# Expert tiles of a graph-plus-mixture kernel: rows scaled by rows and turned by transposing DMAs, gathers issued ahead of additions

## The chip, the cores and the metric

One core of one Trainium2 chip runs the whole program in one launch. The metric is the device time of one execution in microseconds; the median of three runs of the kernel before is 1963.51 us (1962.75 to 1968.17).

## The reference

Three blocks run over the same 6250 nodes of 256 features: a graph attention over 100000 edges, a linear attention, and a mixture of 8 experts of which each node uses 2. The change touches the last block only. Cut to what matters there:

```python
# x: (6250, 256), N = 6250, D = 256, 8 experts, H = 1024
xn = (xt - mu) * rsqrt(var + 1e-5)                 # one row per node
xe = xn[None] * ln_g[:, None] + ln_b[:, None]      # the scale and shift belong to the expert
h = gelu(einsum('end,edh->enh', xe, W1) + b1[:, None])
y = einsum('enh,ehd->end', h, W2) + b2[:, None]
out = (weights[:, :, None] * y[token, its 2 experts]).sum(1)
```

Here `xt` is itself a layer norm of x, so that two norms follow each other; the kernel does both at once and leaves the result in HBM as `xn2_d`.

## The kernel before, in words

The kernel first walks the edges and does the linear attention beside it (up to about 1200 us of the span), then norms all nodes, picks two experts per node and sorts the node-expert pairs by expert. What follows, from about 1322 us on, is the expert loop, and everything below is about it.

The pairs, padded per expert, are cut into FT = 56 tiles of FR = 256 rows; a tile belongs to one expert e. All weights W1 and W2 lie in SBUF, each split into a high and a low float16 part. The activations are split in the same way, so a product takes three float16 products. Even tiles use buffer u = 0 and odd ones u = 1.

For a tile s, in order:

- **GpSimd** (`pool_turn`, the block `@block.gpsimd`) copies the row numbers of turn i into `now` (`places_now`, L857), then issues indirect DMAs. In turn i it adds the gated answers of tile i - 5 to `out` (`add_rows`, L862, two DMAs of 128 rows that read, add and write; the second waits until the first has landed, because the two may hit the same node), gathers the gates of tile i - 2 (`get_gates`, L867, two DMAs) and gathers the 256 normed rows of tile i (`get_rows`, L873, two DMAs into `rows_s`). The order within a turn is: wait until tile i - 2 has been turned by TensorE, wait until tile i - 5 is gated, wait for the additions of the turn before, copy, first addition, gates, second addition, rows.
- **TensorE** (`pe_turn_rows`, L2229) transposes the rows of tile s + 1 in four 128x128 float32 pieces into PSUM bank 6 or 7. In `pe_tile(s)` it does this first, then `pe_up(s)` (L2243, 48 matmuls, W1 times the activations), then `pe_down(s - 1)` (L2263, 48 matmuls, W2).
- **VectorE** (`dve_affine`, L1890) reads that bank and applies the scale and the shift of the expert, which in this layout are one number per partition (`params_s`, loaded and turned at the kernel's start), into `x_f`. **ScalarE** (`act_high`, L1173) casts `x_f` to float16, the high part; VectorE subtracts it (L1895) for the low part. Both go to `x_hl`, which `pe_up` reads.
- ScalarE applies gelu in four quarters (L1152); VectorE splits each quarter into high and low (L1910, L1911) for `pe_down`; VectorE adds the bias b2 to the answer (`dve_answer`, L1924) and ScalarE multiplies it by the gate (`act_gate`, L1165) into `gated_s`.

VectorE's program order in tile s - 1 is: answer of tile s - 3 (the end of its tile s - 2), then affine and low part of tile s, then the four quarters of tile s - 1. ScalarE's is: gate of tile s - 3, high part of tile s, the four gelu quarters. The order is written out by hand on every engine, with semaphores counted by tile. SyncE issues nothing in the loop: its last DMA stores the gates (L728), and then it waits for the end.

Of the kernel before, what the change touches and what calls it, by code (L numbers as in the profile page):

```python
# [5 lines left out]
ACT = mybir.ActivationFunctionType  # L6
# [3 lines left out]
P = 128  # L10
# [26 lines left out]
FR = 2 * P  # L37
# [103 lines left out]
def build(nc, x, src, dst, gnn_w, attn_l, attn_r, gnn_bias, wq, bq, wk, bk, wv, bv, wo, bo,  # L141
          wr, br, ln_g, ln_b, w1, b1, w2, b2, out):
    ctx = ExitStack()
    with ctx:
# [51 lines left out]
        param_rows = first([98, P])  # L196
# [84 lines left out]
        params = sb("params", [P, 98])  # L281
        b1T, gT, bT, bqT = params[:, 0:64], params[:, 64:80], params[:, 80:96], params[:, 96:98]
# [47 lines left out]
        params_s = params[:, 64:96]  # L330
# [28 lines left out]
        x_f = ffn([P, 2, KD, FR])  # L359
# [77 lines left out]
        def high_hots_of(t0, t1):  # L437
# [62 lines left out]
        place_turn, table_turn, map_turn, places_ready = sem("place_turn"), sem("table_turn"), sem("map_turn"), sem("places_ready")  # L500
        now_ready = sem("now_ready")
        adds_ready, tau_turn = sem("adds_ready"), sem("tau_turn")
        rows_got = [sem(f"rows_got{u}") for u in range(2)]
        gates_got = [sem(f"gates_got{u}") for u in range(2)]
        rows_turned, x_turn, x_high, h_made, gelu_ready, h_turn, y_made, y_ready, y_gated, y_added = (
            sem("rows_turned"), sem("x_turn"), sem("x_high"), sem("h_made"), sem("gelu_ready"), sem("h_turn"),
# [9 lines left out]
        RANKS = 21  # L516

# [27 lines left out]
        def _(sp):  # L545
# [180 lines left out]
            load_w2(7)  # L726
            sp.wait_ge(gates_ready, 1)
            sp.dma_start(gate_d.rearrange("(p t) e -> p t e", t=T), gates[:, :, :]).then_inc(gates_out, 16)  # L728

            for g in range(GROUPS - 2, GROUPS):  # L730
                sp.wait_ge(x2_out[g % 2], x2_stored(g))
# [4 lines left out]
        def _(pool):  # L736
# [140 lines left out]
            def pool_turn(i, h):  # L877
                known_i = isinstance(i, int)
                if not known_i or i >= 2:
                    pool.wait_ge(rows_turned, min(i - 1, FT) if known_i else i - 1)  # L880
# [11 lines left out]
                places_now(i, h)  # L892
# [8 lines left out]
                if not known_i or i < FT:  # L901
                    get_rows(h)
# [15 lines left out]
        def _(act):  # L918
# [3 lines left out]
            act.dma_start(param_rows[64:80, :], ln_g.rearrange("e (f p) -> (e f) p", p=P)).then_inc(params_in, 16)  # L922
            act.dma_start(param_rows[80:96, :], ln_b.rearrange("e (f p) -> (e f) p", p=P)).then_inc(params_in, 16)
            act.dma_start(param_rows[96:98, :], bq.rearrange("(f p) -> f p", p=P)).then_inc(params_in, 16)
# [217 lines left out]
            def act_tile(b, u):  # L1142
                s = b * 2 + u
                if not (isinstance(s, int) and s + 1 == FT):
                    act_high(s + 1, 1 - u)
# [30 lines left out]
            act_high(0, 0)  # L1176
# [12 lines left out]
        def _(dve):  # L1189
# [92 lines left out]
            def keep_params():  # L1282
                dve.wait_ge(params_turned, 1)
                dve.tensor_copy(params[:, :], bank[7][:, 0:98]).then_inc(params_kept, 1)
                dve.wait_ge(params_kept, 1)
                dve.tensor_scalar(params_s[:, :], params[:, 64:96], ASCALE, None, ALU.mult).then_inc(params_kept, 1)
# [472 lines left out]
            def find_unused():  # L1759

                in_turn(dve, place_turn, 2 + BLOCKS,
# [3 lines left out]
                dve.wait_ge(place_turn, 5 + BLOCKS)  # L1765
# [57 lines left out]
            in_turn(dve, place_turn, 0,  # L1823
# [3 lines left out]
            dve.wait_ge(place_turn, 2 + BLOCKS)  # L1827
# [7 lines left out]
            in_turn(dve, table_turn, 0,  # L1835
# [4 lines left out]
            dve.wait_ge(table_turn, 3)  # L1840
            dve.wait_ge(owners_made, 1)
            pairs = lambda ap: ap.rearrange("p (s c) -> p s c", c=2)
            in_turn(dve, map_turn, 0,
# [8 lines left out]
            dve.wait_ge(map_turn, 7)  # L1852
# [4 lines left out]
            in_turn(dve, map_turn, 7,  # L1857
# [6 lines left out]
            dve.wait_ge(map_turn, 13)  # L1864
            dve.sem_inc(adds_ready, 1)

            def find_adds():

                dve.wait_ge(unused_placed, 1)
                in_turn(dve, tau_turn, 0,  # L1870
# [9 lines left out]
                dve.wait_ge(tau_turn, 9)  # L1880
# [3 lines left out]
            def dve_affine(s, u, e):  # L1884
# [439 lines left out]
```

## Time and profile before

| | |
|---|---|
| median of three runs | 1963.51 us |
| the profiled execution | 1964.38 us, of which the span is 1962.7 us |
| TensorE matmul busy | 1643.0 us (84% of the span) |
| VectorE busy | 1392.5 us (71%) |
| GpSimd busy | 1301.6 us (66%) |
| ScalarE busy | 1093.9 us (56%) |
| expert loop (from 1322 us) | about 640 us, a third of the span |

"Busy" leaves out register and semaphore instructions and DMA issues of SyncE and ScalarE. GpSimd's indirect DMAs count as busy, since its own cores write the descriptors. The chain of waits is the list of steps that ended last, each with the step that released it.

### The profile page before, as it was taken

To read this page: it belongs to the slowest core of one execution; us is meant where nothing else is said; L and a number is where in the kernel's file an instruction comes from. 1 tells how busy PE (TensorE), PEld (TensorE's weight loads), DVE (VectorE), ACT (ScalarE), POOL (GpSimd) and SP (SyncE) were. 2 spreads that over 40 slices of the span, in tenths; PEclk is the share of its full clock that TensorE was granted. 3 is DMA by queue.
4 is the path that set the end of the run, shared out by engine and by line. 5 is a ranking of instruction groups with operands and counts; after the bars stand their busy time and mean duration, and the time that the engine had idled before them with its cause. 6 is when DMAs were issued, how large, how long until landed. Compare 5 with 4: busy or idle time off the path is not lost.

```text
span 1962.7 us, 50327 instructions
## 1 busy us (share of the span) xinstructions
PE 1643.0 (84%) x11492; PEld 1339.0 (68%) x11493; DVE 1392.5 (71%) x3810; ACT 1093.9 (56%) x3042; POOL 1301.6 (66%) x1235
## 2 busy tenths in 40 slices
PE   6757777788888888888887676928999999999996
PEld 5645455555556777777775455927898989898985
DVE  6656666667777788788878888987666666666663
ACT  4655565666665666666667774673434343434342
POOL 2077777777777777676677774305777777777774
PEclk8979999999998999999999987558999999999998
DMA  7745556565544555444444564742333333333332
GB/s 217 238 118 144 163 155 163 166 178 159 144 118 119 144 145 142 127 136 135 135 131 145 159 200 145 261 168 47 54 48 49 47 51 47 49 47 51 48 49 28
DMA packets 150535, 238.96 MB, mean 122 GB/s; under 512 B 27985, under 2 KB 116169, under 8 KB 149193
## 3 DMA queue, kind: packets, MB, share of 16 engines
q0 software_dynamic: 62784, 134.26, 31.0%
q1 hardware_dynamic: 85944, 103.15, 15.8%
q10 hardware_dynamic: 1744, 0.85, 0.2%
q8 instruction: 23, 0.38, 0.1%
q14 instruction: 40, 0.32, 0.1%
HBM read 181.73 MB, written 56.44 MB: 121 GB/s over the span
## 4 chain that ended last, share of the span: by engine, by line
PE 41%; POOL 18%; issue 15%; DVE 9%; DMA 6%; ACT 5%; DVEq 3%; ACTq 1%; POOLq 1%; SPq 0%
POOL w_s L805 17%; PE bank L2243 15%; PE bank L2263 14%; DMA w_s<-table,w_s 3%; PE bank L2056 3%; PE bank L2129 2%; DVEq L1447 2%; ACT w_s L1028 2%; PE bank L2229 1%; ACT w_s L1001 1%; PE bank L2108 1%; PE bank L2104 1%; DVE w_s L1511 1%; ACTq L983 1%; DVE acc L1674 1%
## 5 line engine op out<-in xcount | busy, mean ns | idle before, releaser
L805 POOL DMA_INDIRECT w_s<-table,w_s x784 | 808.3, 1031 | 280.9 <-issue 237.1
L2056 PE MATMUL bank<-w_s 128*128 128x260 f32 x1952 | 508.7, 406 | 86.2 <-DVE w_s L1511 85.5
L2056 PEld LDWEIGHTS bank<-w_s 128*128 128x128 f32 x1952 | 375.0, 199 | 179.9 <-DVE w_s L1511 98.7
L2243 PE MATMUL bank<-acc,w_s 128*128 128x256 f16 x2688 | 304.1, 273 | 0.0
L2263 PE MATMUL bank<-w_s,acc 128*128 x2688 | 302.6, 273 | 1.1 <-DVE acc L1924 1.1
L2243 PEld LDWEIGHTS bank<-acc,w_s 128*128 x2688 | 263.7, 98 | 30.8 <-issue 0.2
L2263 PEld LDWEIGHTS bank<-w_s,acc 128*128 128x128 f16 x2688 | 262.9, 98 | 31.7 <-issue 1.3
L1001 ACT ACTIVATE w_s<-w_s 128x64 f32 x976 | 260.0, 337 | 33.9 <-ACT w_s L996 0.4
L1511 DVE SCALAR_TENSOR_TENSOR w_s<-w_s 128x256 f32<-128x256 f32 x732 | 268.9, 418 | 10.7 <-ACT w_s L1001 9.9
L862 POOL DMA_INDIRECT out<-mid_g,acc x112 | 202.9, 1812 | 79.1 <-POOL acc L857 47.0
L1008 ACT COPY w_s<-bank 128x512 bf16<-128x512 bf16 x244 | 142.7, 585 | 181.2 <-PE bank L2036 105.9
L1165 ACT ACTIVATE mid_g<-acc 128x256 f32<-128x256 f32 x112 | 50.8, 500 | 301.9 <-DVE acc L1924 187.3
L1478 DVE SCALAR_TENSOR_TENSOR w_s<-w_s,iota 128x512 bf16<-128x512 f32 x244 | 182.6, 748 | 7.0 <-issue 1.6
L1152 ACT ACTIVATE acc<-bank,params 128x256 f32<-128x256 f32 x448 | 172.2, 484 | 17.1 <-issue 14.1
L1911 DVE SCALAR_TENSOR_TENSOR acc<-acc 128x512 f16<-128x512 f32 x224 | 157.0, 701 | 7.7
L996 ACT ACTIVATE w_s<-w_s 128x16 f32<-128x16 f32 x244 | 57.0, 234 | 176.2 <-DVE w_s L1501 175.0
L990 ACT CAST w_s<-w_s 128x512 f32<-128x512 bf16 x244 | 152.2, 624 | 0.0
L2036 PEld LDWEIGHTS bank<-w_s 128*128 128x128 bf16 x976 | 70.8, 101 | 114.0 <-DVE w_s L1478 65.9
L2036 PE MATMUL bank<-w_s 128*128 128x128 bf16 x976 | 99.5, 227 | 52.1 <-DVE w_s L1478 51.8
L867 POOL DMA_INDIRECT acc<-gate_d,acc x112 | 119.5, 1067 | 35.2 <-issue 33.6
L873 POOL DMA_INDIRECT acc<-xn_d,acc x112 | 111.3, 994 | 35.6 <-issue 26.8
L1501 DVE SCALAR_TENSOR_TENSOR w_s<-w_s 128x16 f32<-128x16 f32 x244 | 57.6, 236 | 107.7 <-issue 107.7
(304 smaller groups left out, 2248.9 us busy)
## 6 DMA issues: line engine op xcount, KB each, us to landing
stage<-in_L_ffn_W SPq DMA_DIRECT2D x32, 512.0 KB, 3.3
w_s<-table,w_s POOLq DMA_INDIRECT x784
w_s<-in_x SPq DMA_DIRECT2D x48, 256.0 KB, 4.3
w_s<-xT_d SPq DMA_DIRECT2D x96, 128.0 KB
w_park<-low_g SPq DMA_DIRECT2D x18, 512.0 KB
w_s<-w_park SPq DMA_DIRECT2D x9, 1024.0 KB, 9.2
xn_d<-acc SPq DMA_DIRECT2D x7, 896.0 KB, 4.7
table<-w_s SPq DMA_DIRECT2D x24, 260.0 KB, 3.3
```

The costliest lines, as they stand in the source:

```text
L805: pool.indirect_dma_start(out=ring[:, u, k, :], out_offset=None, in_=table[:, :], in_offset=bass.IndirectOffsetOnAxis(ap=ids[:, h, at + u, ...
L862: pool.indirect_dma_start(out=out[:, :], out_offset=bass.IndirectOffsetOnAxis(ap=now[:, h, sub:sub + 1], axis=0), in_=gated_s[:, 1 - h, su ...
L990: act.copy(hot32[:, k.at % 4, :, :], hot16[:, k.at % 4, :, :]).then_inc(hot32_ready, 1)
L1001: last = act.activation(m[:, e, 0:GD], rows[:, e, 0:GD], ACT.Copy, scale=m[:, e, GD:HC])
L1152: last = act.activation(h32[:, f, :], bank[q][:, (f % 2) * FR:(f % 2 + 1) * FR], ACT.Gelu, bias=b1T[:, bass.ds(e * KF + f, 1)], scale=UNSCALE)
L1478: dve.scalar_tensor_tensor(hot16[:, k.at % 4, :, :], dstT[:, bass.ds(group * SUB, SUB)].unsqueeze(2).to_broadcast([P, SUB, P]), tile_v[:, ...
L1511: last = dve.scalar_tensor_tensor(m[:, e:e + GH, 0:GD], rows[:, e:e + GH, 0:GD], 1.0, m[:, e:e + GH, GD:HC].to_broadcast([P, GH, GD]), ALU ...
L1911: lambda: dve.scalar_tensor_tensor(h_hl[:, u, 1, f0:f1, :], h32[:, f0:f1, :], ASCALE, h_hl[:, u, 0, f0:f1, :], ALU.mult, ALU.subtract))
L2036: last = pe.transpose(turned16[:, s, :], hot16[:, k.at % 4, s, :], ident16[:, :])
L2056: last = pe.matmul(bank[2 + k.at % 2][:, 0:ROW], hot32[:, k.at % 4, s, :], msg[:, k.at % 2, s, :], start=s == 0, stop=s == SUB - 1)
L2243: last = pe.matmul(bank[f // 2][:, (f % 2) * FR:(f % 2 + 1) * FR], w1_s[:, bass.ds(e, 1), k, wh, f * P:(f + 1) * P].rearrange("p a b -> p ...
L2263: last = pe.matmul(bank[4 + sub][:, 0:D], h_hl[:, u, hh, f, sub * P:(sub + 1) * P], w2_s[:, bass.ds(e, 1), f // (KF // 2), wh, f % (KF // ...
```

## The change

The transposes leave TensorE. A tile's rows are scaled and shifted while they still lie with one node per partition, so the expert's 256 scales and 256 shifts are needed as a row that is the same on all partitions: SyncE loads them for each tile from HBM, broadcast to 128 partitions (`load_affine`, two DMAs of 128 KB into `affine`). VectorE multiplies (`tensor_tensor`), adds (`tensor_tensor`), ScalarE makes the high part with a factor of 32 (`activation` Copy, float32 in, float16 out), VectorE makes the low part (`scalar_tensor_tensor`). The result is `rows_hl`, in float16. Then SyncE issues two transposing DMAs (`turn_rows`), each of 128 rows by 512 float16 values (high and low), SBUF to SBUF into `x_hl`. `pe_up` waits for these.

GpSimd's turn has a new order: wait until VectorE has finished with tile i - 2 (its low part), copy, rows of tile i, then wait for the gate of tile i - 5 and the additions of the turn before, first addition, gates, second addition.

At the kernel's start ln_g and ln_b are no longer loaded and turned: ScalarE issues two DMAs fewer there. Several semaphores are merged into `table_turn`, with no change in order.

```diff
+            def load_affine(s, u):
+                e = sp.value_load(ffn_i[0:1, bass.ds(s, 1)], min_val=0, max_val=X - 1)
+                if not (isinstance(s, int) and s < 2):
+                    sp.wait_ge(x_turn, 3 * s - 4)
+                for n, of in enumerate((ln_g, ln_b)):
+                    sp.dma_start(affine[:, u, n, :], of[bass.ds(e, 1), :].to_broadcast([P, D])).then_inc(affine_in[u], 16)
+            def turn_rows(s, u):
+                sp.wait_ge(x_turn, 3 * s + 3)
+                if not (isinstance(s, int) and s < 2):
+                    sp.wait_ge(h_made, 4 * s - 4)
+                sp.sem_inc(carried, 1)
+                for sub in range(2):
+                    sp.dma_start_transpose(x_hl[:, u, :, :, sub * P:(sub + 1) * P].rearrange("p h k r -> p (h k) r"),
+                                           rows_hl[:, u, sub, :, :].rearrange("p h d -> p (h d)")).then_inc(xt_in[u], 16)
+            def sp_tile(s, u):
+                turn_rows(s, u)
+                if not (isinstance(s, int) and s + 2 >= FT):
+                    load_affine(s + 2, u)
...
             def pool_turn(i, h):
-                    pool.wait_ge(rows_turned, min(i - 1, FT) if known_i else i - 1)
+                    pool.wait_ge(x_turn, min(i - 1, FT) * 3 if known_i else i * 3 - 3)
+                if not known_i or i > AHEAD + 1:
+                    pool.wait_ge(y_added, (i - AHEAD - 1) * 32)
...
+                places_now(i, h)
+                if not known_i or i < FT:
+                    get_rows(h)
                 if not known_i or i >= AHEAD:
                     pool.wait_ge(y_gated, i - AHEAD + 1)
                 if not known_i or i > AHEAD:
                     pool.wait_ge(y_added, (i - AHEAD) * 32)
-                places_now(i, h)
+                    pool.sem_inc(carried, 1)
                 if not known_i or i >= AHEAD:
                     add_rows(h, 0)
...
-                if not known_i or i < FT:
-                    get_rows(h)
...
-            act.dma_start(param_rows[64:80, :], ln_g.rearrange("e (f p) -> (e f) p", p=P)).then_inc(params_in, 16)
-            act.dma_start(param_rows[80:96, :], ln_b.rearrange("e (f p) -> (e f) p", p=P)).then_inc(params_in, 16)
...
-            def act_high(s, u):
-                act.wait_ge(x_turn, 2 * s + 1)
+            def act_high(s, u, b):
+                act.wait_ge(x_turn, 3 * s + 2)
                 if not (isinstance(s, int) and s < 2):
-                    act.wait_ge(h_made, 4 * s - 4)
-                act.copy(x_hl[:, u, 0, :, :], x_f[:, u, :, :]).then_inc(x_high, 1)
+                    act.wait_ge(xt_in[u], b * 32)
+                act.activation(rows_hl[:, u, :, 0, :], rows_s[:, u, :, :], ACT.Copy, scale=ASCALE).then_inc(x_high, 1)
...
-            def dve_affine(s, u, e):
-                dve.wait_ge(rows_turned, s + 1)
-                if not (isinstance(s, int) and s < 2):
-                    dve.wait_ge(x_high, s - 1)
-                for k in range(KD):
-                    last = dve.tensor_scalar(x_f[:, u, k, :], bank[6 + u][:, k * FR:(k + 1) * FR],
-                                             params_s[:, bass.ds(e * KD + k, 1)], params_s[:, bass.ds(e * KD + k + KD * X, 1)],
-                                             ALU.mult, ALU.add)
-                last.then_inc(x_turn, 1)
+            def dve_affine(s, u, b):
+                def factor(n):
+                    return affine[:, u, n, :].unsqueeze(1).to_broadcast([P, 2, D])
+                dve.wait_ge(rows_got[u], (b + 1) * 32)
+                dve.wait_ge(affine_in[u], (b + 1) * 32)
+                dve.tensor_tensor(rows_s[:, u, :, :], rows_s[:, u, :, :], factor(0), ALU.mult).then_inc(x_turn, 1)
+                dve.wait_ge(x_turn, 3 * s + 1)
+                dve.tensor_tensor(rows_s[:, u, :, :], rows_s[:, u, :, :], factor(1), ALU.add).then_inc(x_turn, 1)
                 dve.wait_ge(x_high, s + 1)
-                dve.tensor_tensor(x_hl[:, u, 1, :, :], x_f[:, u, :, :], x_hl[:, u, 0, :, :], ALU.subtract).then_inc(x_turn, 1)
+                dve.scalar_tensor_tensor(rows_hl[:, u, :, 1, :], rows_s[:, u, :, :], ASCALE, rows_hl[:, u, :, 0, :],
+                                         ALU.mult, ALU.subtract).then_inc(x_turn, 1)
...
-            def pe_turn_rows(s, u, b):
-                pe.wait_ge(rows_got[u], (b + 1) * 32)
...
-                last.then_inc(rows_turned, 1)
-            def pe_up(s, u):
+            def pe_up(s, u, b):
                 e = pe.value_load(ffn_i[0:1, bass.ds(s, 1)], min_val=0, max_val=X - 1)
-                pe.wait_ge(x_turn, 2 * s + 2)
+                pe.wait_ge(xt_in[u], (b + 1) * 32)
...
             def pe_tile(b, u):
                 s = b * 2 + u
-                if not (isinstance(s, int) and s + 1 == FT):
-                    pe_turn_rows(s + 1, 1 - u, b + u)
-                pe_up(s, u)
+                pe_up(s, u, b)
```

## Rows read from the trace of the kernel before

**Rows 1.** The page, parts 1 and 2: TensorE's busy share, DMA share in 40 slices.

```profile
PE 1643.0 (84%) x11492; PEld 1339.0 (68%) x11493; DVE 1392.5 (71%) x3810; ACT 1093.9 (56%) x3042; POOL 1301.6 (66%) x1235
...
DMA  7745556565544555444444564742333333333332
```

**Rows 2.** Chain of waits in the expert loop: start us, us, what.

```profile
1525.62 5.24 PE bank L2243 x48
1530.87 5.24 PE bank L2263 x48
1536.11 0.44 PE bank L2229 x4
```

**Rows 3.** Busy time of each engine in a stretch: stretch, its us, PE, PEld, DVE, ACT, POOL.

```profile
1500.00:1718.30 218.30, 218.30 (x2002) 196.56 (x2001) 136.92 (x261) 91.81 (x220) 159.42 (x141) 1.00 0.32 49
```

**Rows 4.** Timeline of one tile: start us, us, engine, line; idle before in brackets.

```profile
1514.11 0.60 PE L2229 MATMUL bank<-ident,acc 128*128 128x128 f32 x4
...
1514.52 0.76 DVE L1924 SCALAR_TENSOR_TENSOR acc<-bank,stage 128x256 f32<-128x256 f32 x2 [2.11 <-PE bank L2263]
...
1515.82 1.00 DVE L1890 TENSOR_SCALAR acc<-bank,params 128x256 f32<-128x256 f32 x2 [0.54 <-issue]
...
1516.93 0.62 ACT L1173 CAST acc<-acc 128x512 f16<-128x512 f32 x1 [0.45 <-DVE acc L1890]
1517.58 0.69 DVE L1895 TENSOR_TENSOR acc<-acc 128x512 f16<-128x512 f32 x1 [0.77 <-ACT acc L1173]
...
1522.62 0.69 DVE L1911 SCALAR_TENSOR_TENSOR acc<-acc 128x512 f16<-128x512 f32 x1
...
1525.35 0.76 DVE L1924 SCALAR_TENSOR_TENSOR acc<-bank,stage 128x256 f32<-128x256 f32 x2 [2.03 <-PE bank L2263]
```

**Rows 5.** Timeline at the kernel's start: VectorE on two float32 operands of 512.

```profile
11.22 0.69 DVE L1264 TENSOR_TENSOR acc<-w_s,acc 128x512 f32<-128x512 f32 x1
```

**Rows 6.** SyncE's DMAs: issue of two (timeline), then KB and us to landing.

```profile
12.99 0.84 SPq L555 DMA_DIRECT2D xT_d<-w_s  x2
...
xT_d<-w_s SPq DMA_DIRECT2D x48, 128.0 KB, 3.3
...
out<-acc SPq DMA_DIRECT2D x6, 896.0 KB, 10.1
```

**Rows 7.** GpSimd's timeline: starts of four turns, and one late second addition.

```profile
1387.73 0.21 POOL L857 COPY acc<-low_g 128x6 int32 x1
...
1397.83 0.58 POOL L857 COPY acc<-low_g 128x6 int32 x1
...
1516.75 0.19 POOL L857 COPY acc<-low_g 128x6 int32 x1 [0.31 <-ACT mid_g L1165]
...
1527.58 0.19 POOL L857 COPY acc<-low_g 128x6 int32 x1 [0.22 <-ACT mid_g L1165]
...
1632.93 1.62 POOL L862 DMA_INDIRECT out<-mid_g,acc  x1 [1.41 <-issue]
```

**Rows 8.** Timeline of the loop's start, tiles 0 and 1.

```profile
1328.10 1.09 PE L2229 MATMUL bank<-ident,acc 128*128 128x128 f32 x4 [9.17 <-DMA acc<-xn_d,acc]
...
1331.22 0.69 DVE L1895 TENSOR_TENSOR acc<-acc 128x512 f16<-128x512 f32 x1 [0.74 <-ACT acc L1173]
...
1332.14 6.92 PE L2243 MATMUL bank<-acc,w_s 128*128 128x256 f16 x48
...
1339.87 5.41 PE L2243 MATMUL bank<-acc,w_s 128*128 128x256 f16 x48
```

**Rows 9.** GpSimd's timeline at the end: turns 59 and 60.

```profile
1941.67 0.18 POOL L857 COPY acc<-low_g 128x6 int32<-128x6 int32 x1 [3.00 <-ACT mid_g L1165]
1942.69 1.59 POOL L862 DMA_INDIRECT out<-mid_g,acc  x1 [0.83 <-POOL acc L857]
...
1951.15 0.19 POOL L857 COPY acc<-low_g 128x6 int32<-128x6 int32 x1 [2.39 <-DMA out<-mid_g,acc]
1952.13 1.57 POOL L862 DMA_INDIRECT out<-mid_g,acc  x1 [0.80 <-POOL acc L857]
```

More of the change, by code:

```diff
@@ L195, in build @@
         edge_rows_f = first([112, 14, P])
-        param_rows = first([98, P])
+        param_rows = first([66, P])
         attn_b = first([P, 2, D])
@@ L280, in build @@
         iota = sb("iota", [P, 256])
-        params = sb("params", [P, 98])
-        b1T, gT, bT, bqT = params[:, 0:64], params[:, 64:80], params[:, 80:96], params[:, 96:98]
+        params = sb("params", [P, 66])
+        b1T, bqT = params[:, 0:64], params[:, 64:66]
         eps_c = sb("eps_c", [P, 1])
@@ L358, in build @@
         rows_s = ffn([P, 2, 2, D])
-        x_f = ffn([P, 2, KD, FR])
+        rows_hl = ffn([P, 2, 2, 2, D], F16)
+        affine = ffn([P, 2, 2, D])
         x_hl = ffn([P, 2, 2, KD, FR], F16)
@@ L516, in build @@
         RANKS = 21
+        PLACED = 2 + BLOCKS
         block = ctx.enter_context(nc.Block())
@@ L726, in _ @@
             load_w2(7)
+            def load_affine(s, u):
[12 more added lines that the diff above has]
+                                           rows_hl[:, u, sub, :, :].rearrange("p h d -> p (h d)")).then_inc(xt_in[u], 16)
+            sp.wait_ge(table_turn, PLACED + 3)
+            sp.wait_ge(owners_made, 1)
+            for g in range(GROUPS - 2, GROUPS):
+                sp.wait_ge(xn2_out[g % 2], stored(g))
+            for u in range(2):
+                load_affine(u, u)
             sp.wait_ge(gates_ready, 1)
             sp.dma_start(gate_d.rearrange("(p t) e -> p t e", t=T), gates[:, :, :]).then_inc(gates_out, 16)
+            def sp_tile(s, u):
+                turn_rows(s, u)
+                if not (isinstance(s, int) and s + 2 >= FT):
+                    load_affine(s + 2, u)
+            for u in range(2):
+                sp_tile(u, u)
+            with sp.Fori(1, FT // 2 - 1) as b:
+                for u in range(2):
+                    sp_tile(b * 2 + u, u)
+            for u in range(2):
+                sp_tile(FT - 2 + u, u)
             for g in range(GROUPS - 2, GROUPS):
@@ L1822, in _ @@
             std_groups(1)
-            in_turn(dve, place_turn, 0,
+            in_turn(dve, table_turn, 0,
                     lambda: dve.memset(tb_d[:, :], 0.0),
@@ L1951, in turn_params @@
             def turn_params():
-                pe.wait_ge(params_in, 4 * 16)
-                pe.transpose(bank[7][:, 0:98], param_rows[:, :], ident[0:98, 0:98]).then_inc(params_turned, 1)
+                pe.wait_ge(params_in, 2 * 16)
+                pe.transpose(bank[7][:, 0:66], param_rows[:, :], ident[0:66, 0:66]).then_inc(params_turned, 1)
             def turn_pair(i, u):
@@ L2221, in _ @@
             last.then_inc(owners_made, 1)
-            def pe_turn_rows(s, u, b):
-                pe.wait_ge(rows_got[u], (b + 1) * 32)
-                if not (isinstance(s, int) and s < 2):
-                    pe.wait_ge(x_turn, 2 * s - 3)
-                for k in range(KD):
-                    for sub in range(2):
-                        last = pe.transpose(bank[6 + u][:, k * FR + sub * P:k * FR + (sub + 1) * P],
-                                            rows_s[:, u, sub, k * P:(k + 1) * P], ident[:, :])
-                last.then_inc(rows_turned, 1)
-            def pe_up(s, u):
+            def pe_up(s, u, b):
                 e = pe.value_load(ffn_i[0:1, bass.ds(s, 1)], min_val=0, max_val=X - 1)
-                pe.wait_ge(x_turn, 2 * s + 2)
+                pe.wait_ge(xt_in[u], (b + 1) * 32)
                 for f in range(KF):
```

52 lines of the change are left out of this document (24 added, 28 removed).

## The prediction

> **What bounds the kernel now.** I began with the page's busy shares and its 40 slices [rows 1]: TensorE has 84% of the span, and in the last 13 slices, the expert loop, the DMA engines are a third busy. The change touches only that loop, so the second view was the chain of waits there. The reader is to see that it holds nothing but TensorE [rows 2]: 5.24 us of up matmuls, 5.24 us of down matmuls and 0.44 us of transposes, together 10.92 us a tile, again and again from tile 2 to the last. The busy times of a stretch of 20 tiles confirm it [rows 3]: PE is busy 218.3 of 218.3 us at a granted clock of 1.00 (2.4 GHz), VectorE 136.9 (6.85 a tile), ScalarE 91.8 (4.6), GpSimd 159.4 (8.0). The third view, the timeline of one tile, gives the order of the others inside these 10.92 us [rows 4]. The fourth, GpSimd's timeline, shows how near to the bound it is [rows 7]: from one copy to the next 10.83 us (1516.75 to 1527.58), of which only 0.22 us waited for a gate. So two engines are close to the pace, and one of them is relieved.
>
> **The transposes on TensorE go.** Of the 56 tiles' transposes, those of tiles 0 and 1 lie in the start. From the up matmuls of tile 1 on (1339.87, [rows 8]) 53 more groups at 0.437 us (10.92 less 2 x 5.24, [rows 2]) stand in line: 23.2 us off, if nothing else is late. The pace would be 10.48 us.
>
> **VectorE.** Before: two ops of 0.50 and one of 0.69 a tile. After: a multiply and an add of 512 float32, for which the same form at the kernel's start took 0.69 [rows 5], and a low part that I take at the 0.69 of the splitting op in the quarters [rows 4]. It adds 2 x 0.69 - 1.00 = 0.4 us: 7.2 of 10.48 busy. On its timeline, counted from the start of the transposes at 1514.11, the answer ends at +1.17, the affine started at +1.71 after 0.54 us of issue (the register load for the expert's column, which the new form has not), the high part ran from +2.82 to +3.44 and the low part ended at +4.16 [rows 4]. New: multiply +1.3 to +2.0, add +2.05 to +2.75, high part +2.85 to +3.5, low part to +4.2. A wash: the 0.54 us that go pay for the longer ops. If half of them stay as waits the low part ends at +4.5. The quarters then end at +9.2, where the cover was 2.03 us of idle [rows 4]; at the new pace 1.4 us are left. VectorE stays off the path.
>
> **ScalarE.** A copy with a factor instead of a cast, 512 elements both: 0.62 us, no change. It now waits for the landing of the transposes of tile s - 2, with the gelu quarters queued behind; that landing is a whole tile old.
>
> **The transposing DMAs are the new link.** The up matmuls of tile s start one pace after the mark from which I counted, at +10.48, and SyncE can issue at +4.2. So the two DMAs have 6.3 us, from the first's issue to the second's landing, before TensorE waits. The trace has no transposing DMA. The nearest row is a pair of 128 KB from SBUF, issued in 0.84 us together and landing in 3.3 us [rows 6]: 0.42 + 3.3 = 3.7 us. That is the lower end. The upper end, far off, is the slowest landing of any SyncE transfer, 10.1 us for 896 KB [rows 6]. I take 4.5 us, the near row plus 0.8 us for a heavier issue and for sharing the engines with GpSimd's traffic; TensorE then does not wait, with 1.8 us to spare. Past 6.3 us each microsecond is paid in all 54 tiles; past 6.7 us (10.92 - 4.2) the loop is slower than before.
>
> The Trainium skill speaks against this step. Its page "VectorE: DVE Perf Modes", section "The three transpose paths", gives 390 ns for one 128x128 block of 2-byte values on TensorE and 1309 ns by the DMA crossbar, and advises TensorE where a PSUM result will do. By an estimate from that page, eight blocks a tile one after the other would take 10.5 us and the loop would be far slower; this trace bears out only the TensorE side, 0.437 us for four float32 blocks. The same skill's page "DMA: Bandwidth & Descriptors", section "Latency and other measured facts", gives 261 GB/s for transposing DMAs, which by estimate is 1 us for both. No run here shows either yet.
>
> **SyncE's other work.** Two loads of 128 KB a tile are issued behind the transposes and have a whole tile before VectorE needs them, so they cost nothing on the path; uncovered, as in the start, they land in some 4 us. The waits of SyncE (for the low part of s and for up matmuls of s - 2) have only these loads queued behind. The 256 KB of loads and 256 KB of transposes a tile come on top of the 49 GB/s of the loop [rows 3] and make it about double. What this does to GpSimd's landings is the second rival.
>
> **GpSimd.** The same six indirect DMAs and one copy, in another order. The new first wait, for the low part of tile i - 2, opens at +4.2; before, a turn began with the gate, at about +2.6 (1516.75, [rows 7]). Behind it are the rows, both additions and the gates. The rows are still 10 us early, the additions some 1.9 us later than before but a tile ahead of the gate that needs their buffer. Its own cycle: 10.83 less 0.22 of waiting is 10.6, and while it was behind in the loop's start it ran 10.10 us from copy to copy (1387.73 to 1397.83, [rows 7]). The mean of these two is 10.35, just under 10.48. I cost the order at nothing; if 10.6 holds it is the bound, which is the second rival. In the end it gains: the copy and its 0.83 us until the DMA now lie ahead of the wait for the gate in turn 59 and ahead of the landing in turn 60 [rows 9], 2 x 0.9 = 1.8 us off.
>
> **Start of the loop.** The rows of tile 0 have landed at 1328.1, and the low part ended at 1331.91 with the transposes and affine in between [rows 8]. New: four ops from 1328.3, 0.69 + 0.69 + 0.62 + 0.69 and gaps, to 1331.3; plus 4.5 us of transposing DMA, 1335.8 for the first matmul instead of 1332.14. That is 3.7 us late; the transposes that stood before tile 1's matmuls (0.64 and a short gap) go, so tile 1's start moves from 1339.87 to 1342.7: 2.9 us on. By the ends 3.7 and 10.1 us this is 2.1 and 8.5. The two ScalarE issues that go at the kernel's start I cost at 0: VectorE waits there for a later transfer.
>
> **Sum.** -23.2 + 2.9 - 1.8 = -22.1 us, against the profiled execution's 1964.4 us (span 1962.7): 1942.3. The median of the runs is 0.9 us under that execution, which makes 1941.4. I say 1942 us.
>
> **Rivals.** (a) *The transposing DMAs are late, slower than before.* For it: no such DMA is in the trace, two follow each other, and they share 16 engines with additions; the chain low part, issue, landing, matmul has no second buffer of time beyond 6.3 us. Against: the volume is small and the near row is 3.7. The point from which it decides is 6.7 us. At 7.5 us the pace is 11.7 and the time 1964 + 54 x 0.8 + 5 = 2012; at 7.0 it is 1983; at 10.1 it is 2154. (b) *They take by block what a DMA's issue takes.* Eight blocks of 0.42 us and a landing of 3.3 are 6.7 us [rows 6]: a pace of 10.9, so the 0.44 us come back as a wait and the time is about 1967 with the start. (c) *GpSimd becomes the bound.* For it: 10.6 us of own work in the locked pattern, and second additions that already come late now and then because the first has not landed (1.41 us, [rows 7]), with twice the DMA traffic to come. Against: it ran 10.1 when it was behind. At 10.65 us, 50 turns times 0.17 is 8.5 us of the gain lost: 1951; at 10.8 about 1958. (d) The change doesn't relieve TensorE at all: excluded, since its instructions go and it is 100% busy.
>
> **Chances.** Forecast 0.47 (1937 to 1950); (c) 0.15, two thirds of it still faster; (b) with its neighbourhood of 6.3 to 6.8 us 0.10, of which 0.03 faster; (a) 0.28. A measurement of this kernel tells 0.3%, 5.9 us, from no change. Faster: 0.47 + 0.10 + 0.03 = 0.60; within: 0.05 + 0.07 = 0.12; slower 0.28. The range reaches from 1936 (landing at 3.7 us, 2.1 at the start, and a little from the kernel's start) into (a) up to a landing of 7.0 us: 1984, which leaves out about 0.2.
>
> **What would show it.** Chain of waits in the loop: only 5.24 and 5.24, no L2229. If (a) or (b), PE idle before each tile's first up matmul, released by the transposing DMA, and PE busy under 100%. If (c), ScalarE's gate waiting for the additions and GpSimd with no idle before its copies, PE waiting behind VectorE's answer. The first up matmul at 1336 or thereabouts tests the 4.5 us at once; the low part at +4.2 tests VectorE; GpSimd's last two turns without a gap of 0.8 test the end. I am wrong if issue to landing of the pair exceeds 6.3 us or GpSimd's cycle exceeds 10.5.

## The result and the profile after

The changed kernel takes 2026.8 us (median of 4 runs, 2024.3 to 2037.8) against 1963.3: ratio 1.033, interval 1.029 to 1.036. It is slower by 63 us where 21 us of gain were forecast. Its profiled execution took 2037.8 us (span 2036.1), the slowest of the four. In it the time from GpSimd's first copy of the expert loop to the end of the span grew from 640.2 to 710.7 us; the 3.0 us that are left lie before the loop, where the profiled executions of before, changed and e1 to e4 scatter by as much (first copy at 1320.1 to 1325.4).

First the busy shares, to be held against [rows 1], and the stretch of [rows 3]:

```profile
PE 1636.1 (80%) x11268; PEld 1315.9 (65%) x11269; DVE 1412.5 (69%) x3809; ACT 1084.5 (53%) x3042; POOL 1294.6 (64%) x1235
...
DMA  7745555656444545544445638545454544555452
...
1500.00:1718.30 218.30, 194.49 (x1737) 169.05 (x1736) 130.19 (x234) 79.18 (x198) 139.95 (x126) 0.99 0.50 87
```

TensorE has lost its 224 transposes (4 in each of 56 tiles; 11492 matmul instructions before, 11268 now), but is now idle for 24 of 218 us, and every other engine is less busy than before. No engine is the bound by its own work: the loop waits. The DMA engines are half busy instead of a third and move 87 instead of 49 GB/s.

The waits between 1500 and 1950 us (who waited for what: us in total, times, longest):

```profile
ACT mid_g L1204 <- DMA out<-mid_g,acc: 286.2, 37, 8.6
DVE acc L1932 <- ACT acc L1212: 158.7, 37, 5.2
POOL out L900 <- DMA out<-mid_g,acc: 79.2, 41, 3.0
...
PE bank L2269 <- DMA acc<-acc: 51.6, 34, 2.6
```

ScalarE's gate waits in every tile, and GpSimd's next addition too, for the landing of an addition to `out` (the moment when all of a DMA's data is written and its semaphore has the full count); VectorE's low part waits for ScalarE; TensorE's up matmuls wait, last in the row, for the transposing DMAs. The timeline of one tile shows the order (to be held against [rows 4, 7]):

```profile
1605.48 1.97 POOL L900 DMA_INDIRECT out<-mid_g,acc  x1 [0.49 <-issue]
1606.03 0.36 SPq L736 DMA_DIRECT2D acc<-in_L_ffn_ln_g  x1
...
1606.87 0.79 POOL L895 COPY acc<-low_g 128x6 int32 x1
1606.95 5.41 PE L2269 MATMUL bank<-acc,w_s 128*128 128x256 f16 x48 [1.13 <-DMA acc<-acc]
1607.29 0.76 DVE L1961 SCALAR_TENSOR_TENSOR acc<-bank,stage 128x256 f32<-128x256 f32 x2 [0.26 <-issue]
1607.96 0.68 DVE L1928 TENSOR_TENSOR acc<-acc 128x512 f32<-128x512 f32 x1
...
1609.83 0.95 POOL L911 DMA_INDIRECT acc<-xn_d,acc  x1 [0.30 <-issue]
1612.07 0.91 ACT L1204 ACTIVATE mid_g<-acc 128x256 f32<-128x256 f32 x2 [7.56 <-DMA out<-mid_g,acc]
1612.76 1.62 POOL L900 DMA_INDIRECT out<-mid_g,acc  x1 [1.98 <-DMA out<-mid_g,acc]
1612.88 0.61 ACT L1212 ACTIVATE acc<-acc 128x512 f16<-128x512 f32 x1
...
1613.53 0.69 DVE L1932 SCALAR_TENSOR_TENSOR acc<-acc 128x512 f16<-128x512 f32 x1 [4.16 <-ACT acc L1212]
1614.43 2.59 SPq L744 DMA_TRANSPOSE acc<-acc  x2
...
1617.50 1.89 POOL L900 DMA_INDIRECT out<-mid_g,acc  x1 [0.57 <-issue]
...
1619.14 5.41 PE L2269 MATMUL bank<-acc,w_s 128*128 128x256 f16 x48 [1.54 <-DMA acc<-acc]
```

Read it as a ring. The second addition of a tile starts at 1605.48. GpSimd issues the next rows behind it and then stands for 1.98 us until that addition has landed; only then goes the first addition of the next tile, at 1612.76. From there to the second is 4.74 us, which is the landing of the first beside the gates. 7.28 + 4.74 = 12.0 us is the pace of this tile; over 40 tiles it is 12.2. Before, the same two steps were 5.8 and 5.0 us (additions at 1517.78, 1522.80 and 1528.60), and GpSimd's wait before an addition was put down to a landing only once between 1500 and 1950 us. The chain of waits has the landing itself: the second addition takes 6.4 us from its start.

```profile
1605.48 6.46 DMA out<-mid_g,acc
1617.50 6.42 DMA out<-mid_g,acc
```

The landing events that the traces keep say more (medians of 40 tiles). In the kernel before, a first addition lands after 4.1 us and a second one after 3.9; in the changed kernel the first takes 4.0 us, as before, and only the second takes 6.5. The next addition starts some 0.8 us behind a landing, so the ring is two landings and twice 0.8 us. What stands beside the second addition and not beside the first is in the timeline: SyncE issues its two loads at 1606.03 and 1606.49, right behind the addition of 1605.48, and its two transposing DMAs, issued from 1602.29 on, are still under way (the up matmuls of 1606.95 wait for them). In 37 of 40 tiles the loads follow a second addition, in the median by 0.9 us. The ring keeps it so: the landing opens ScalarE's gate, behind it come the high part, the low part and the transposing DMAs, and behind these the loads, once more beside a second addition.

The gate of tile s - 3 needs the buffer of tile s - 5, so it opens with the same landing (1612.07), and behind it on ScalarE stands the high part of tile s, then the low part, the transposes and the up matmuls. The 4.7 us from the transposes' issue (1614.43) to the matmuls (1619.14) only look like the cause: they are the last link of a chain that started late (e1 below has the same DMAs without the wait).

The start, against [rows 8], and the end, against [rows 9]:

```profile
1325.42 0.19 POOL L895 COPY acc<-low_g 128x6 int32<-128x6 int32 x1 [65.14 <-DVEq L1890]
...
1332.79 0.69 DVE L1928 TENSOR_TENSOR acc<-acc 128x512 f32<-128x512 f32 x1 [1.65 <-DMA acc<-xn_d,acc]
...
1334.96 0.69 DVE L1932 SCALAR_TENSOR_TENSOR acc<-acc 128x512 f16<-128x512 f32 x1 [0.76 <-ACT acc L1212]
...
1335.75 2.64 SPq L744 DMA_TRANSPOSE acc<-acc  x2
...
1340.46 7.28 PE L2269 MATMUL bank<-acc,w_s 128*128 128x256 f16 x48 [18.57 <-DMA acc<-acc]
...
2020.85 1.56 POOL L900 DMA_INDIRECT out<-mid_g,acc  x1 [2.90 <-DMA out<-mid_g,acc]
2021.83 0.78 POOL L895 COPY acc<-low_g 128x6 int32<-128x6 int32 x1
2025.36 1.57 POOL L900 DMA_INDIRECT out<-mid_g,acc  x1 [2.75 <-DMA out<-mid_g,acc]
```

### The profile page after: what moved, and what is told of

It reads as the page before. It is cut to its first block, busy times and chain, and to the rows that moved or that the text cites. A ratio compares the mean times of both kernels' runs of the same rounds, so it can differ in the third digit from the quotient of the medians.

```text
span 2036.1 us, 50464 instructions
## 1 busy us (share of the span) xinstructions
PE 1636.1 (80%) x11268; PEld 1315.9 (65%) x11269; DVE 1412.5 (69%) x3809; ACT 1084.5 (53%) x3042; POOL 1294.6 (64%) x1235
## 4 chain that ended last, share of the span: by engine, by line
issue 23%; DMA 23%; POOL 22%; PE 11%; DVE 9%; ACT 6%; DVEq 4%; ACTq 2%; POOLq 1%; SPq 0%
DMA out<-mid_g,acc 18%; POOL w_s L843 16%; POOL acc L905 4%; PE bank L2092 3%; DVEq L1484 2%; PE bank L2165 2%; DMA w_s<-table,w_s 2%; POOL out L900 2%; ACT w_s L1067 2%; ACT w_s L1040 1%; PE bank L2144 1%; DVE w_s L1548 1%; PE bank L2140 1%; ACTq L1022 1%; ACT w_s L1029 1%
## 5 line engine op out<-in xcount | busy, mean ns | idle before, releaser
L2269 PE MATMUL bank<-acc,w_s 128*128 128x256 f16 x2688 | 311.2, 277 | 85.1 <-DMA acc<-acc 85.0
L900 POOL DMA_INDIRECT out<-mid_g,acc x112 | 195.0, 1741 | 153.5 <-DMA out<-mid_g,acc 124.3
L1932 DVE SCALAR_TENSOR_TENSOR acc<-acc 128x512 f16<-128x512 f32 x56 | 38.8, 692 | 200.9 <-ACT acc L1212 200.9
L1948 DVE SCALAR_TENSOR_TENSOR acc<-acc 128x512 f16<-128x512 f32 x224 | 157.8, 705 | 7.7
L905 POOL DMA_INDIRECT acc<-gate_d,acc x112 | 114.6, 1023 | 34.1 <-issue 34.1
```

The costliest lines, as they stand in the source:

```text
L900: pool.indirect_dma_start(out=out[:, :], out_offset=bass.IndirectOffsetOnAxis(ap=now[:, h, sub:sub + 1], axis=0), in_=gated_s[:, 1 - h, su ...
L905: pool.indirect_dma_start(out=gate_s[:, 1 - h, sub, :], out_offset=None, in_=gate_d[:, :], in_offset=bass.IndirectOffsetOnAxis(ap=now[:, h ...
L2269: last = pe.matmul(bank[f // 2][:, (f % 2) * FR:(f % 2 + 1) * FR], w1_s[:, bass.ds(e, 1), k, wh, f * P:(f + 1) * P].rearrange("p a b -> p ...
```

## The experiments

Two groups of runs don't compare in their times: e5 to e16 ran where the kernel before takes 2341 to 2345 us, because its edge walk is some 380 us longer. The record names chip 5 for e1 to e12 and chip 7 for e13 to e16, so what makes the walk longer is not known. The expert loop of the changed kernel is the same in both (710.7 us in the first group, 710.1 in the second), so beside the ratio each run is told by its loop: from GpSimd's first copy to the end of the span. Each loop is that of one profiled execution; kernels that ran more than once in the second group differ by up to 8 us from themselves. The kernel before was not profiled in the second group; e7, whose loop is 640.5, is the nearest to it. Start is from the first copy to the first up matmul, body from there to the last matmul's end, tail what is left.

| kernel | ratio to before (interval) | loop us | start | body | tail |
|---|---|---|---|---|---|
| before | 1 | 640.2 | 9.7 | 613.9 | 16.7 |
| changed | 1.033 (1.029 to 1.036) | 710.7 | 15.0 | 671.0 | 24.7 |
| e1 loads gone | 0.995 (0.994 to 0.996) | 631.0 | 15.6 | 593.4 | 22.1 |
| e2 plain copies | 1.004 (1.002 to 1.007) | 647.9 | 13.2 | 607.4 | 27.3 |
| e3 changed, old order | 1.011 (1.008 to 1.014) | 660.5 | 15.2 | 622.4 | 22.8 |
| e4 before, new order | 1.000 (0.999 to 1.001) | 640.5 | 9.7 | 614.5 | 16.4 |
| e5 distinct rows | 1.006 (1.000 to 1.012) | 659.1 | 13.6 | 623.4 | 22.1 |
| e6 before + loads | 1.001 (0.996 to 1.007) | 642.9 | 9.7 | 615.3 | 17.9 |
| e7 before + transposes | 1.002 (0.996 to 1.007) | 640.5 | 9.7 | 614.1 | 16.7 |
| e8 before + both | 0.998 (0.992 to 1.005) | 659.9 | 9.8 | 633.2 | 16.9 |
| e9 load at a change | 1.005 (1.001 to 1.009) | 661.1 | 15.3 | 623.5 | 22.2 |
| e10 the same, old order | 1.003 (1.000 to 1.005) | 646.9 | 15.3 | 608.1 | 23.5 |
| e11 changed again | 1.033 (1.025 to 1.041) | 710.1 | 15.7 | 669.4 | 24.9 |
| e12 distinct rows again | 1.008 (1.004 to 1.012) | 661.7 | 13.7 | 627.3 | 20.7 |
| e13 = e10 again | 1.000 (0.996 to 1.003) | 638.8 | 14.8 | 601.5 | 22.4 |
| e14 = e9 again | 1.008 (1.004 to 1.012) | 653.5 | 14.7 | 618.4 | 20.4 |
| e15 distinct rows, third | 1.005 (1.001 to 1.009) | 656.5 | 13.6 | 621.9 | 21.0 |
| e16 one load a tile | 1.004 (1.001 to 1.008) | 652.2 | 14.2 | 618.5 | 19.6 |

**e1, without the loads.**

```diff
-                if not (isinstance(s, int) and s + 2 >= FT):
-                    load_affine(s + 2, u)
...
-                dve.wait_ge(affine_in[u], (b + 1) * 32)
+                dve.wait_ge(affine_in[u], 32)
```

> The changed kernel without the per-tile loads of scale and shift: only tiles 0 and 1 load them, all later tiles use these two (so 54 of 56 tiles use the scales of the wrong expert; time only). Theory A, GpSimd's additions land late (6.4 us after the start of the second, against 3.6 in the quiet tail of the kernel before) because the loads are issued right beside the second addition: landing back to about 4.5 us, pace 10.5 to 10.8 us instead of 12.1, time 1945 to 1960. Theory B, the transposing DMAs delay the additions: pace stays at about 11.5 to 12, time 2000 to 2025. Theory C, the new order of GpSimd's turn costs it: no change, 2020 to 2030.

1952.8 us, 9 us under the kernel before, as theory A had it. With 54 pairs of loads 79.7 us of loop go: the whole loss of 70.5 us and 9 more. The second additions land after 4.1 us again, not 6.5. The loop now is what the prediction described (busy times of the stretch; then GpSimd's additions and the up matmuls on the timeline):

```profile
1500.00:1718.30 218.30, 218.30 (x2003) 195.66 (x2001) 148.98 (x271) 94.25 (x228) 166.35 (x145) 1.00 0.46 76
```

```profile
1703.63 1.62 POOL L898 DMA_INDIRECT out<-mid_g,acc  x1 [0.30 <-issue]
1703.99 5.40 PE L2267 MATMUL bank<-acc,w_s 128*128 128x256 f16 x48
...
1708.38 1.62 POOL L898 DMA_INDIRECT out<-mid_g,acc  x1 [0.51 <-issue]
...
1714.13 1.62 POOL L898 DMA_INDIRECT out<-mid_g,acc  x1 [0.30 <-issue]
1714.47 5.40 PE L2267 MATMUL bank<-acc,w_s 128*128 128x256 f16 x48
```

TensorE is 100% busy at 10.48 us a tile, and the transposing DMAs hide.

**e2, plain copies.**

```diff
-                    sp.dma_start_transpose(x_hl[:, u, :, :, sub * P:(sub + 1) * P].rearrange("p h k r -> p (h k) r"),
-                                           rows_hl[:, u, sub, :, :].rearrange("p h d -> p (h d)")).then_inc(xt_in[u], 16)
+                    sp.dma_start(x_hl[:, u, :, :, sub * P:(sub + 1) * P].rearrange("p h k r -> p (h k) r"),
+                                 rows_hl[:, u, sub, :, :].rearrange("p h (k r) -> p (h k) r", r=P)).then_inc(xt_in[u], 16)
```

> The changed kernel with the two transposing DMAs replaced by plain DMAs of the same bytes, same buffers, same 256 byte pieces, same semaphores (the values are not transposed; time only). Theory B, the transposing form is what hurts (its issue of 1.3 us each and its load on the engines): time 1945 to 1965, DMA share well below 0.50. Theory A, the loads of scale and shift: 2015 to 2027. Theory C, the order: 2015 to 2027. If it is only bytes, whatever their kind, then about a third to a half of the 63 us goes: 1995 to 2010.

1968.9 us: 58 us come back, against 74 without the loads, though the DMA share of the stretch went up from 0.50 to 0.58, not down as theory B had it. The time lies in no theory's range, nearest to theory B's, and the loads are all there. So neither kind alone makes the loss.

```profile
1500.00:1718.30 218.30, 213.72 (x1938) 187.53 (x1936) 145.45 (x262) 89.60 (x226) 158.71 (x141) 1.00 0.58 97
```

**e3 and e4, GpSimd's order alone.**

```diff
-                places_now(i, h)
-                if not known_i or i < FT:
-                    get_rows(h)
                 if not known_i or i >= AHEAD:
                     pool.wait_ge(y_gated, i - AHEAD + 1)
...
+                places_now(i, h)
...
                     add_rows(h, 1)
+                if not known_i or i < FT:
+                    get_rows(h)
```

(e3; e4 is the reverse edit in the kernel before, with one wait for the gates of tile i - 5 ahead of the copy.)

> The changed kernel with GpSimd's turn in its old order (gate of i - 5, additions, gates, rows last). Theory C, the order costs: the rows no longer stand between the second addition and the next first one, 1955 to 1985. Theories A and B, traffic: the landing of the second addition still bounds the turn; 2020 to 2035, and perhaps worse, since the rows of a tile then come later.

> The kernel before with only GpSimd's turn in the new order (rows ahead of the additions), plus one wait for the gates of tile i - 5 that the order needs. Theory C: it already has the late additions, 1975 to 2020. Theories A and B: within 3 us of the kernel before, and up to 2 us faster at the end, where the copy stands ahead of the waits (1960 to 1966).

The order costs the kernel before nothing (1962.4 against 1962.0, as theories A and B had it) and the changed kernel 50 us of loop (e3's 1981 us is in theory C's range). So it costs only together with the traffic. The traces say how: in both orders the rows and the copy stand between a second addition and the next first one, but the old order moves the loads away from the additions. In e3 they follow a second addition in 7 of 40 tiles, else a first one, 2.4 us behind it in the median; the second additions land after 4.0 us in the median. Where a load does start beside an addition, as here at 1643.19, that one is late too, and the next copy waits for it. That the order acts by this alone is argued from the traces, not shown by an experiment.

```profile
1642.08 1.62 POOL L900 DMA_INDIRECT out<-mid_g,acc  x1 [2.75 <-issue]
1643.19 0.35 SPq L736 DMA_DIRECT2D acc<-in_L_ffn_ln_g  x1
...
1648.15 0.19 POOL L895 COPY acc<-low_g 128x6 int32 x1 [1.71 <-DMA out<-mid_g,acc]
```

The rows that now come last are late for VectorE (waits between 1500 and 1880 us):

```profile
DVE acc L1925 <- DMA acc<-xn_d,acc: 30.5, 16, 4.3
POOL out L900 <- DMA out<-mid_g,acc: 28.9, 18, 2.9
```

**e6, e7, e8, the traffic alone on the kernel before.** SyncE issues the same DMAs into buffers that nobody reads (e8; e6 has the loads only, e7 the transposes only).

```diff
+            def sp_tile(s):
+                e = sp.value_load(ffn_i[0:1, bass.ds(s, 1)], min_val=0, max_val=X - 1)
+                sp.wait_ge(x_turn, 2 * s + 2)
...
+                for sub in range(2):
+                    sp.dma_start_transpose(turned_d[:, :, sub * P:(sub + 1) * P], iota[:, :].bitcast(F16)).then_inc(base_read, 16)
...
+                for n, of in enumerate((ln_g, ln_b)):
+                    sp.dma_start(affine[:, n, :], of[bass.ds(e, 1), :].to_broadcast([P, D])).then_inc(bias_in, 16)
```

> The kernel before plus the loads of scale and shift a tile from SyncE, into a buffer that nobody reads. What traffic of this kind costs by itself on GpSimd's additions: theory that each kind alone stays under the cliff (one addition's landing hidden behind the gathers), pace still 10.92, time 1960 to 1968. Theory that the loads alone are what delays the additions past the pace: 11.3 us or more a tile, 1980 to 2010.

> The kernel before plus two transposing DMAs a tile of 128x512 float16 from SyncE, of a constant into a buffer that nobody reads. Theory that each kind alone stays under the cliff: 1960 to 1968. Theory that the transposing DMAs slow the additions by themselves: 1980 to 2010; without the loads the changed kernel ran at 10.48 us a tile, which speaks for the first.

> The kernel before plus both kinds of DMA from SyncE, in the changed kernel's order (two transposes, then two loads), all into buffers that nobody reads; TensorE still transposes and GpSimd's turn is in its old order. If the loss is nothing but the additions of GpSimd landing late under this traffic, the kernel before must lose too: 1975 to 2010 (old order; the changed kernel in the old order took 1981). If it needs the new data path (TensorE waiting for the transposing DMAs), it stays at 1960 to 1968.

The ratios are too wide to show this: the executions of the kernel before alone scatter from 2320 to 2364 us here. The loops, of one execution each, are 642.9, 640.5 and 659.9 us against 640.2 in the first group. By them each kind alone is free or nearly so and both together cost 20 us, in a kernel whose data path is untouched. These 20 us rest on that one trace: the ratio of e8 is 0.998 with an interval that ends at 1.005, 13 us, while the medians differ by 15 us (2356 against 2341). The waits of e8's trace are of the expected kind (1780 to 2300 us; in e6 and e7 the same wait has 13.7 and 10.0 us; in e8 TensorE's transposes also stand 9.4 us for rows, in the others not at all):

```profile
POOL out L881 <- DMA out<-mid_g,acc: 29.9, 14, 3.8
```

One thing e6 does not test: its loads start 4.0 us behind a second addition, in the median, when that has all but landed.

**e5, e12, e15, the same bytes from other rows,** with e11, the changed kernel, beside e12.

```diff
-                for n, of in enumerate((ln_g, ln_b)):
-                    sp.dma_start(affine[:, u, n, :], of[bass.ds(e, 1), :].to_broadcast([P, D])).then_inc(affine_in[u], 16)
+                for n in range(2):
+                    sp.dma_start(affine[:, u, n, :], x[bass.ds((e * 2 + n) * P, P), :]).then_inc(affine_in[u], 16)
```

> The changed kernel with the two loads a tile taken from 128 different rows of x instead of one row of ln_g or ln_b repeated for 128 partitions: same bytes, same pieces of 1 KB, same waits (the tiles are scaled with wrong numbers; time only). Theory A1, the loads hurt because 128 pieces read one and the same kilobyte of HBM: the additions land about as early as without the loads, 1950 to 1965. Theory A2, they hurt by their bytes and pieces, wherever these come from: 2020 to 2030, as the changed kernel (2027).

> The changed kernel with the same bytes a tile loaded from 128 different rows of x instead of one row repeated (tiles scaled with wrong numbers; time only), now beside the changed kernel on the same chip. By the trace of its first run the loop takes 659 us, so 1978 to 1985: theory A1, about two thirds of the loss is the repeated reading of one kilobyte, the rest is bytes. Theory A2, bytes only: equal to the changed kernel within 0.5%.

> The changed kernel once more, unaltered, beside the others on the same chip: 2020 to 2035, and from the loop's first copy to the end 700 to 711 us (before: 640).

> The changed kernel with the same bytes loaded from 128 different rows of x (tiles scaled with wrong numbers; time only). Loop 640 to 662 us against 711 of the changed kernel if the repeated kilobyte is what hurts; 700 or more if bytes do.

Loops of 659.1, 661.7 and 656.5 us against 710.1: about 50 of the 70 us go when the 128 partitions read 128 kilobytes instead of one kilobyte 128 times. The times say the same: e12 took 2364 us beside 2417 of e11. GpSimd then stands for an addition once in 520 us where it stood 41 times in 450. This is theory A1.

A rival is left: in these three most loads start 4.7 us behind a second addition, where the changed kernel has them at 0.9 us, so perhaps they only miss it. The traces speak against it. Take the additions beside which a load was issued (from 1.0 us before to 1.5 us after their start) and the others, among 96 of each trace:

| kernel | landing beside a load, us | other landings, us |
|---|---|---|
| changed | 6.5 (45) | 4.0 (51) |
| e11 changed again | 6.5 (44) | 4.0 (50) |
| e2 plain copies | 5.2 (45) | 3.9 (51) |
| e3 changed, old order | 5.4 (16) | 4.0 (80) |
| e8 before + both | 5.5 (20) | 4.0 (73) |
| e9 load at a change | 6.0 (11) | 3.9 (85) |
| e6 before + loads | 4.5 (20) | 3.9 (76) |
| e5 distinct rows | 3.9 (35) | 3.9 (57) |
| e16 one load a tile | 3.9 (24) | 3.9 (72) |

(Medians, number of additions in brackets. The traces of the second group lack some of the landing events.) Loads from distinct rows do not delay an addition even beside it. And the packets of the loads, 1 KB each, are themselves slower with the repeated row: over 400 us of loop their mean is 102 ns in the changed kernel, 103 in e11 and 104 in e6, against 51 to 53 ns in e5, e12 and e15.

The 16 to 21 us that stay are largely of another kind (waits, 1802 to 2322 us of e15):

```profile
DVE acc L1961 <- remote: 65.6, 23, 5.7
POOL out L900 <- DMA out<-mid_g,acc: 2.8, 1, 2.8
```

VectorE's answer starts 0.25 us behind the last down matmul in every tile looked at in the first group; in e5, e12, e15 and e16 it starts 1.3 to 1.6 us behind it in the median and up to 5.4 us, with its matmuls done, and the releaser is given as another core or an unknown queue. The chain of waits puts 5.6% of 520 us on such waits in e5 and 4.7% in e15, 29 and 24 us, which is about what their bodies lie above e1's (623.4 and 621.9 us against 593.4). They are in e9, e11 and e14 too, less, and hardly or not at all in the others. No run without the loads was made in this group, so what distinct rows cost by themselves is not known, and what these waits are stays open.

**e16, half the dose.**

```diff
-                for n, of in enumerate((ln_g, ln_b)):
+                for n, of in enumerate((ln_g,)):
...
-                dve.wait_ge(affine_in[u], (b + 1) * 32)
+                dve.wait_ge(affine_in[u], (b + 1) * 16)
```

> The changed kernel with one load a tile, the scale; the shift is loaded once for two experts and kept (tiles shifted with a wrong expert's numbers; time only). Half the dose of repeated reads. If the additions' landing grows with the loads and only what exceeds the pace is paid, clearly less than half of the 80 us between no loads (631) and two (711): 632 to 655. If each load costs the same, 671.

652.2 us, in the expected range: of 80 us between none and two loads, 58 go with the second load. The 21 us that stay over e1 can't be put on the first one: e1 is of the first group, the chain of waits of e16 has 4.0% of 520 us, 21 us, on the unknown waits of e15, and an addition beside the load lands after 3.9 us like every other (table above). The packets of the one load take 59 ns in the mean, though it repeats its row as before. So it takes the two repeated loads together; half the dose does far less than half the harm.

**e9, e10, e13, e14, the whole result kept.** VectorE makes a flag a tile, SyncE loads only where the expert of tile s + 2 is another than that of tile s: 18 pairs of loads instead of 56.

```diff
+            def load_changed(s, u):
+                sp.load([same_r], same_i[0:1, bass.ds(s - 2, 1)])
+                with sp.If_eq(same_r, 0):
+                    load_affine(s, u)
+                with sp.If_eq(same_r, 1):
+                    sp.wait_ge(x_turn, 3 * s - 4)
+                    sp.sem_inc(affine_in[u], 32)
```

> The changed kernel, whole result kept, but SyncE loads scale and shift for tile s + 2 only where its expert differs from that of tile s (a table of flags made by VectorE, a branch on SyncE); of 54 loads in the loop some 14 are left. Theory that the loads are what pushes the additions over the pace: close to the run without them (1953): 1950 to 1958, faster than the kernel before by 0.3 to 0.6%. Theory that only the HBM row or the order matters: above 1970.

> The same with GpSimd's turn in its old order. With the loads nearly gone the order should matter little: 1948 to 1960. If the rows then come too late for VectorE, as they did with the loads (30 us of waits in 380 us), 1962 or more, and the new order has its use.

> The changed kernel with loads only where the expert changes and GpSimd's turn in the old order, once more. By its first trace the loop takes 647 us (before: 640): 1963 to 1972, the same as before or 0.3% slower. If its stalls were that chip's, 1950 to 1960.

> The changed kernel with loads only where the expert changes, new order, once more. First trace: loop 661 us, with 35 us of stalls of ScalarE that no semaphore explains. Theory that these belong to that chip: loop 632 to 640, 1952 to 1962. Theory that they belong to the kernel: 1975 to 1985.

With the new order 661.1 and 653.5 us, which misses the 631 of e1 and the hope of 1950 to 1962; e14's ratio of 1.008 would be 1979 us in the first group, what was expected if the stalls belong to the kernel. With the old order 646.9 and 638.8, a draw with the kernel before (1.003 and 1.000). There the body is shorter (608.1 and 601.5 us against 613.9, though not e1's 593.4), and the start and the tail, 5 to 7 us longer each, take nearly all of it back, or more. No version that keeps the whole result was shown to beat the kernel before.

## Why the prediction was wrong

**The step that failed** is the one on GpSimd and SyncE's other work: "I cost the order at nothing", and loads that "cost nothing on the path". The price was put on the path of the loaded data, where it is indeed nothing, and only a 10.65 to 10.8 us pace was allowed in rival (c). Measured: 12.2 us, since the landing of a second addition beside the loads went from 3.9 to 6.5 us, and the two additions of a tile must land one after the other. The mechanism of rival (c) was the right one, mis-sized, and its reading of [rows 7] was wrong: the addition that came 1.41 us late there has "issue" as its releaser, and the trace has the one before it landed after 4.2 us, as in the other tiles. What the kernel before did show is that each second addition starts some 0.8 us behind the first one's landing, 5.0 us after the first one's start, in a turn of 10.9. No row had what doubling the traffic, or loading a repeated row beside an addition, does to a landing; the range should have held it.

**A time near rival (a)'s came, by another way, so that is luck.** It had 2012 us at a landing of 7.5 us, but the pair of transposing DMAs took 4.7 us from issue to matmul, in the start (1335.75 to 1340.46) as in the loop; 4.5 was forecast. e1 shows them hidden. The estimate from the Trainium skill, page "VectorE: DVE Perf Modes", section "The three transpose paths", at 1309 ns a block would have made it 10.5 us for eight: this trace does not agree for blocks that share one DMA, 8 blocks in 4.7 us with issue and landing. Nor does 0.437 us for four float32 blocks on TensorE bear out the 390 ns for one block that the Trainium skill's page has there, as the prediction says it does. The estimate of 1 us for both from the Trainium skill's page "DMA: Bandwidth & Descriptors", section "Latency and other measured facts", leaves out the issue, 2.6 us for the pair.

**TensorE's term was right where nothing else bound**: -23.2 us forecast in the body, -20.5 in e1 (613.9 to 593.4), whose body also holds the start's shift between tiles 0 and 1.

**VectorE's and ScalarE's terms were right**: 0.69 us each for multiply, add and low part, 0.63 for the high part; 7.2 us a tile forecast, 7.15 in e1 (148.98 us in 20.8 tiles).

**The start** was forecast 3.7 us late for the first matmul, it was 5.3 (15.0 after the copy against 9.7). The rows of tile 0 landed late, VectorE stood 1.65 us for them at 1332.79. With loads from distinct rows the start is 13.6 to 13.7, so the loads of tiles 0 and 1 seem to have a part in it.

**The end** was forecast 1.8 us shorter and is 8.0 longer (5.4 in e1). The copy does lie ahead of the wait (2021.83), as forecast. But GpSimd arrives later: in the kernel before, its turns 57 to 60 waited 2.3 to 3.0 us for a landing or the gate (59 and 60 in [rows 9]) and three additions started behind the last matmul; in the changed one five did, 4.4 to 4.7 us apart.

## What to carry to other kernels

Additions that must land one after the other are a clock of their own: work out two landings a tile against the pace, with the landing under the new traffic and not that of a quiet stretch, before anything is added to the DMA engines. Two broadcasts of one row of HBM to all partitions, repeated every tile beside transposing DMAs, were dearer here for their neighbour than the same bytes from many rows; load such rows when they change (18 pairs instead of 56 took 49 to 57 us off the loop), and look where in the tile the loads fall. And reordering that only moves slack (e4: no cost) can decide what meets what under a later traffic (e3: 50 us), so try an order together with the traffic it will meet.

## What the runs showed of the hardware

One repeated kilobyte: 128 pieces of 1 KB from one row of HBM, in two loads a tile beside transposing DMAs, cost the loop 70 us, net of what the change gains. With them an addition of 128 rows landed after 6.5 us instead of 4.0, with plain copies in place of the transposing DMAs after 5.2, with the loads alone after 4.5, with distinct rows or with one repeated load after 3.9. The loads alone on the kernel before left its loop at 642.9 us and the transposing DMAs alone at 640.5, against 640.2 of the first group. The packets of the repeated pair took 102 to 104 ns in the mean, those of distinct rows 51 to 53, those of a single repeated load 59. Why two repeated rows at once are slow and one is not, and whether their lying in two small tensors matters, no run separates. A pair of transposing DMAs of 128x512 float16 holds SyncE's queue for 2.6 us; a pair of plain DMAs of the same pieces 1.3 us (e2).
